# Two clears of 780 columns per group on GpSimd, between the row gathers of both edge stages

## What is computed

```python
# layer 0: attention over edges
h = (x @ W).reshape(N, H, C)
e = jax.nn.leaky_relu(a_src[src] + a_dst[dst], NEG_SLOPE)
e_exp = jnp.exp(e - e_max[dst])
out = jax.ops.segment_sum(h[src] * alpha[:, :, None], dst, num_segments=N)
# layer 1: messages from four products, weights from an MLP of the edge's 8 numbers
w = silu(edge_scalars @ fc_w1 * ...) @ fc_w2 * ...
xg0, xg1 = y0[edge_src], y1[edge_src]
agg = jax.ops.segment_sum(mids, edge_dst, num_segments=n)
```

## Time and profile before

| | us |
|---|---|
| median of 3 runs | 4372.39 |
| lowest, highest | 4357.10, 4376.29 |
| the profiled execution | 4357.34 |
| its span, first to last instruction | 4355.6 |
| mean granted TensorE clock | 0.833 |

### The profile page before, as it was taken

The page is one execution under the profiler, slowest core; times in us unless marked ns, Lnnn a source line. Parts: engine busy times, 40 slices in busy tenths (PEclk is TensorE's granted clock), DMA queues, the critical chain, the costliest instruction groups (busy, mean ns, idle before and its releaser), DMA issues. The chain is left out here.

```text
span 4355.6 us, 80354 instructions
## 1 busy us (share of the span) xinstructions
PE 3384.6 (78%) x22728; PEld 2463.9 (57%) x22728; DVE 2266.0 (52%) x6165; ACT 1433.0 (33%) x4367; POOL 1898.9 (44%) x2266
## 2 busy tenths in 40 slices
PE   6577777766777787999588888778887777878679
PEld 4466666655666665888344444444444444446568
DVE  5455555555555575766344444444444444456732
ACT  5122222222222173333133333333333333314612
POOL 3655656666556310111444444444444444451144
PEclk9678888888888898999678778887777877879889
DMA  6333333333333464322322222222222222223511
GB/s 196 109 88 84 86 85 91 87 85 87 84 87 93 105 191 127 92 85 75 91 66 67 64 65 67 68 67 64 65 65 66 66 64 66 67 80 97 172 42 48
DMA packets 239107, 375.93 MB, mean 86 GB/s; under 512 B 88190, under 2 KB 145606, under 8 KB 238762
## 3 DMA queue, kind: packets, MB, share of 16 engines
q0 software_dynamic: 89712, 230.26, 19.2%
q1 hardware_dynamic: 147482, 140.83, 11.6%
q10 hardware_dynamic: 1696, 2.62, 0.2%
HBM read 310.75 MB, written 62.84 MB: 86 GB/s over the span
## 5 line engine op out<-in xcount | busy, mean ns | idle before, releaser
L1980 POOL DMA_INDIRECT e_rows<-tab,e_ix x828 | 788.4, 952 | 1006.6 <-DVE e_msg L2154 679.5
L586 POOL DMA_INDIRECT e_rows<-tab,e_ix x830 | 794.0, 957 | 533.5 <-issue 254.2
L2222 PE MATMUL e_pU<-e_msg,e_oh 128*32 128x128 f32 (+1 forms) x6672 | 557.8, 337 | 312.2 <-issue 307.3
L2152 DVE TENSOR_TENSOR e_msg<-e_pW,e_rows 128x256 f32<-128x256 f32 x417 | 176.8, 424 | 925.3 <-remote 680.6
L2222 PEld LDWEIGHTS e_pU<-e_msg,e_oh 128*32 128x32 f32 x6672 | 297.7, 120 | 553.5 <-issue 495.0
L981 PE MATMUL e_pU<-e_ohp,e_rows 128*128 128x128 f32 x3340 | 531.8, 321 | 89.8 <-issue 85.9
L981 PEld LDWEIGHTS e_pU<-e_ohp,e_rows 128*128 128x128 f32 x3340 | 503.3, 235 | 103.6 <-issue 96.9
L2208 PE MATMUL e_pW<-e_w,e_hT 64*128 64x256 f32 x1668 | 396.8, 513 | 51.2 <-DVE e_msg L2154 22.4
L2154 DVE TENSOR_TENSOR e_msg<-e_pW,e_rows 128x384 f32<-128x384 f32 x834 | 422.2, 548 | 0.0
L695 ACT CAST e_ohT<-e_pT 64x640 bf16<-64x640 f32 x167 | 114.6, 686 | 900.0 <-remote 511.6
L2038 ACT COPY e_us<-e_pU 96x512 f32<-96x512 f32 x139 | 80.9, 582 | 752.4 <-PE e_pU L2222 653.3
(11 more groups left out here) (453 smaller groups left out, 5713.5 us busy)
## 6 DMA issues: line engine op xcount, KB each, us to landing
e_rows<-tab,e_ix POOLq DMA_INDIRECT x1658
xnT<-f_xnT SPq DMA_DIRECT2D x25, 250.0 KB, 3.2
e_xk<-xnT SPq DMA_DIRECT2D x25, 250.0 KB
xnT<-b_xT SPq DMA_DIRECT2D x25, 250.0 KB, 3.0
m_xnT<-xnT SPq DMA_DIRECT2D x25, 250.0 KB
xnT<-m_xT SPq DMA_DIRECT2D x25, 250.0 KB, 2.7
ffn_norm<-xnT SPq DMA_DIRECT2D x25, 250.0 KB
tab<-f_hrow SPq DMA_DIRECT2D x25, 227.5 KB
```

Source lines behind the costliest of these rows:

```text
L586: nc.gpsimd.indirect_dma_start(out=rows[:, s, j, :], out_offset=None, in_=env["tab0"], in_offset=bass.IndirectOffsetOnAxis(ap=at[:, j:j + ...
L1980: nc.gpsimd.indirect_dma_start(out=rows[:, r % PER, j, :], out_offset=None, in_=env["tab1"], in_offset=bass.IndirectOffsetOnAxis(ap=at[:, ...
L2222: last = nc.tensor.matmul(u8[:, 0:8:2, :] if c == 0 else u8[:, 1:2 + 2 * c:2 * c, :], oh[:, r % 2, ST * i + j, c, :], m[:, 0:4, :] if c == ...
```

## The change

In both edge stages GpSimd clears a tile of its own, `pace`, 128 partitions by 780 float32 columns, ahead of the first gather of each group (j = 0) and ahead of the fourth (j = 3). Nobody reads `pace`. Each clear increments a semaphore `s_pace`, and ahead of each clear but the first stands a hold until the clear before it is done. The clear for j = 0 stands behind the holds for the group's buffer, ahead of the hold for tile 0; the one for j = 3 stands ahead of the holds for tiles 3 and later, of the index copy and of the fourth gather. The two semaphores are reset with the others of their stage. Nothing is removed.

```diff
@@ edges0 @@
+        pace = sb("pace", [P, 780])
...
-        s_eq = sem("e0_equal")
+        s_eq, s_pace = sem("e0_equal"), sem("e0_pace")
...
                             hold(pool, s_acc, g - SLOTS + 1)
                         for j in range(GT):
+                            if j in (0, 3):
+                                if lo >= 1 or j == 3:
+                                    hold(pool, s_pace, 2 * g + j // 3)
+                                nc.gpsimd.memset(pace[:, :], 0.0).then_inc(s_pace, 1)
                             if lo >= 1:
                                 for i in ((j,) if j < 3 else range(3, GT) if j == 3 else ()):
                                     hold(pool, s_row[i], 16 * g)
@@ edges1 @@
+        pace = sb("pace", [P, 780])
...
+        s_pace = sem("e1_pace")
...
                             hold(pool, s_msg, PAIRS * (g - PER + 1))
                         for j in range(T1):
+                            if j in (0, 3):
+                                if lo >= 1 or j == 3:
+                                    hold(pool, s_pace, 2 * g + j // 3)
+                                nc.gpsimd.memset(pace[:, :], 0.0).then_inc(s_pace, 1)
                             if lo >= 1:
                                 for i in ((j,) if j < 3 else range(3, T1) if j == 3 else ()):
                                     hold(pool, s_row[i], 16 * g)
```

More of the change, by code:

```diff
@@ L1111, in edges0 @@
         window_loop(env, iota, one_pass, s_row, GROUPS,
-                    s_dw + [s_ix, s_oh, s_eq, s_T, s_ohT, s_E, s_lg, s_ed, s_p, s_ohp, s_acc, s_add,
+                    s_dw + [s_pace, s_ix, s_oh, s_eq, s_T, s_ohT, s_E, s_lg, s_ed, s_p, s_ohp, s_acc, s_add,
                             s_xk, s_kv, s_sq, s_ss, s_sd, s_kvn, s_ks, s_qw, s_wq, s_bp, s_kvb, s_pb,
@@ L2315, in edges1 @@
         window_loop(env, env["iotaW"][:, :], one_pass, s_row, GROUPS1,
-                    s_es + [s_ix, s_T, s_esT, s_F, s_h, s_W, s_msg, s_eq, s_oh, s_acc, s_us, s_flip, s_add,
+                    s_es + [s_pace, s_ix, s_T, s_esT, s_F, s_h, s_W, s_msg, s_eq, s_oh, s_acc, s_us, s_flip, s_add,
                             s_wk, s_xk, s_kv, s_read, s_ab, s_sd, s_ri, s_vs, s_gram, s_cp, s_wf, s_dT, s_M, s_m1, s_G, s_wl],
```

## The result

The changed kernel takes **4133.65 us** in the median of 4 runs (4120.31 to 4135.94); the kernel before took 4367.62 us beside it (4 runs). The ratio is 0.9459 with a 95% interval of 0.9428 to 0.949: 5.4% faster. The profiled execution took 4133.68 us with a span of 4131.9 us, 223.7 us less than before.

The account below looks back on a forecast made before the run. TensorE was taken as the busiest engine, held by "issue" stalls while row gathers are in flight. 4357.3 - 168 - 33 - 20 = 4136 us, plus 15 for the runs' median, said as 4150 us; range 3980 to 4390.

Parts of the forecast that it names:

- What GpSimd has to spare, and the clear's price: First stage, GpSimd: 1.8 of 8.2 us a group free; a clear costs 746 ns, making a group 7.75 us.
- The first stage, 33 us: First edge stage: relief of 0 to 66 us, where GpSimd stops it; half taken, 33 us.
- The waits, at nothing: GpSimd's waits on the pace semaphore are long met, and later gathers are wanted some four groups later: cost nil.
- The second stage's stall, 168 us: TensorE's "issue" idle in the second edge stage: relief of 0 to 337 us; half taken, 168 us.
- the clock, 20 us: TensorE's clock in the second stage rises as stalls get rarer: 0 to 142 us, 20 us taken.
- all of it: Upper bound of the second stage's relief: all 337 us of TensorE's idle time there.
- The `tensor_scalar`, at nothing: VectorE's L826 in the first stage could wait for clears: at most 125 us, 11 us on average, nothing taken.
- The cause: TensorE runs on a store of instructions that drains while row gathers are in flight; inferred from timing.
- Full relief: Rival: the break refills the store and almost no stall is left in either edge stage, 3920 us; chance 0.20.
- Only moved: Rival: each TensorE stall shifts 1.1 us and keeps its length, 4372 us; chance 0.17.
- GpSimd bound: Rival: GpSimd bounds the first stage, with no relief, at 8.93 us a group, +121 us, 4493 us; chance 0.11.

Follow-up runs that it names:

- first stage alone: Both clears in the first edge stage only, none in the second, against the kernel before: 4247.40 us, 0.9836.
- the first set: First of three sets of follow-up runs, each beside the kernel before, which took 4314.50 us in it.
- the third set: Last of three sets of follow-up runs, each beside the kernel before, which took 3344.69 us in it.
- the form with two inputs: VectorE's minimum as scalar_tensor_tensor, on the kernel with both clears in the first stage, the fourth gather's in the second (4110.78 us): 4106.39 us.
- the kernel with no-ops alone: The kernel before with 20 no-ops more on TensorE in each group of the second edge stage: 3341.09 us, 0.9989.
- The kernel with the double break: Against the kernel before: both clears in the first stage; in the second, two clears in a row ahead of the fourth gather only: 3965.44 us, 0.9084.
- the last kernel: Against the kernel before: both clears in the first stage; in the second, clears ahead of the third and fifth gathers: 3627.48 us, 1.0842.

## Why the prediction was right, and where it was not

The forecast was 4150 us and the runs gave 4134, inside the range. Direction and place of the gain were right, and so was the break inside the burst as what brings it. The terms of the second stage were each off and their errors cancelled, which is luck. By its steps:

- **What GpSimd has to spare, and the clear's price.** Right. A clear was priced at 746 ns and takes 758 to 763; the inner break is 1.05 us for 1.1. The group of 7.75 us on GpSimd showed as 7.72 us a group where the stage ran at its pace (first stage alone).
- **The first stage, 33 us.** It was 36, at 8.0 us a group with GpSimd 80% busy (forecast 8.0 and over 75%). "Issue" there fell by about 110 us (269 to 159), three times the gain; the rest went to TensorE's wait for one-hots, 124 to 185 us. The half that I took had no row behind it, and in the first set the same clears brought 64 us, nearly the whole 66 that I had as the bound, at GpSimd's pace; in the changed kernel GpSimd still had 52 us of idle time ahead of its clears. That 33 fits 36 is luck too.
- **The waits, at nothing.** No run changed them alone. Ahead of the clears GpSimd's idle time in the second stage is mostly for VectorE's messages (354 us), that is the buffer it waited for before (679.5 us). The later gathers are felt a little: VectorE's messages wait 60.2 us for gathered rows and not 25.3, but TensorE's wait for the messages did not grow (20.1 to 8.4 us).
- **The second stage's stall, 168 us, and the clock, 20 us.** Together 188, and the stage gave 187. Each was mis-sized. "Issue" fell by 213 us, not by 168. The idle time of TensorE fell by 47 us only, since ScalarE's late copy took 155 us. And the busy term was 139 us and not 20: it stood at the upper bound that I had worked out, 142 us, though for another reason in part. The rise of the clock from 0.79 to 0.82 gives, as an estimate, 1458 x (1 - 0.79/0.82) = 53 us; that the starved matmuls overlap again gives most of the rest, 99 us at the sums alone (the two shares cover each other in part). So the step that failed is the assumption that a stall is what "issue" shows and that its fall is gain. The bound of "all of it" failed with it: I had 337 us (the rows of the trace add up to 334), and without the stall the second stage is 701 us shorter, 1120.6 for 1821.6 us.
- **The `tensor_scalar`, at nothing.** Right, with the wait longer than I thought: a mean of 411 ns for 236, 29 us in all against my 11, and one of 1475 ns. Removing it changed nothing. In the third set it reached 138 us of VectorE's time, over the 125 us that I gave as its bound, and there too GpSimd set the stage's length. The Trainium skill (SBUF — State Buffer, section "Who interferes with whom") states a rule for it: a `tensor_scalar` in a 2-port mode and an instruction of GpSimd contend, and the one that comes second is blocked for the whole of the other. The runs agree: the form with two inputs takes 182 ns beside the same clears. The long ones exceed one clear; clear and index copy, which stand back to back, and its own 177 ns make 0.77 + 0.20 + 0.18 = 1.15 us, near the 1.18 us that is the median where the mean is 1091 ns.
- **The cause.** That TensorE runs on a store of instructions that drains was inferred, and no run shows it. What the runs show is wider. "Issue" on TensorE is one face of it, the "remote" waits of VectorE and ScalarE another. In the kernel with no-ops alone, in the third set, neither engine has such a row in the second stage: all of them vanish together. The same section of the Trainium skill says that "PE and ACT never wait on anyone". It speaks of the ports of SBUF; taken as my rival took it, that gathers cannot hold TensorE back, it fails in the first two sets and fits the third. Whether the engines waited at a port or for something else no run shows.
- **The rivals.** "Full relief" priced the stall at 337 us of idle plus 50 of clock, 3920 us. The kernel with the double break took 398 us off (4363.84 to 3965.44), and without the stall the kernel takes 3345 us, some 1000 less: there was far more to gain than my full relief held. "Only moved" is refuted by the kernel with the fourth gather's clear alone, in time and in "issue" (29.4 us at the sums), though a part of the stall did move, to ScalarE. "GpSimd bound" came true in the last kernel, with its mechanism and at +283 us, in the set without the stall. The changed kernel itself was not run there; the inner break alone (with the no-ops, which cost nothing by themselves) cost 3.5% there.

**What stays open.** Why gathers hold back the engines in some sets and not in another; whether descriptors, bytes or instruction traffic does it; whether two breaks are better than one long one where the stall is; and whether an idle pause of GpSimd would do as well as a clear, which was not tried. The first and the third set carry the same chip number, 15; whether it was the same chip is not known, so it isn't shown that the difference is one between chips.

## What to carry to other kernels

Where engines wait for "issue" or "remote" while indirect gathers are in flight, break the burst inside, not ahead of it, and try a longer break: 1.05 us inside took 5 to 6% off, 1.9 us in the second stage took 9%, and the clear ahead of the burst nothing by itself. Such a stall is larger than its idle rows: look at the busy time of the same matmuls and at the next engine's "remote" waits, and expect the wait to move there. Measure in more than one place and at more than one time before keeping such a pause. Where the stall is absent the clears cost their own time on a GpSimd that is then the bound: 3.5% with one a group, 8.4% with two.

## What the runs showed of the hardware

- The same program took 4368, 4315 and 4364 us in the median beside the changed kernel and in the first two sets, and 3345 us in the third, within 0.7% in each. Outside the two edge stages the executions agree: from the last gather of the one to the first of the other it is 626 us in the kernel before and 620 us in the one with no-ops alone. In the second edge stage the difference is 13.2 against 8.1 us a group, with TensorE at a clock of 0.79 against 0.95.
- While row gathers follow each other every 1.25 us, TensorE (9 matmuls in 5 us), ScalarE (2.2 us late at 2824.58) and VectorE (until 2819.03) can all stand still, and go on as the gathers end or pause; not in the third set.
- The granted clock follows the stall in the second stage: 0.79 with it, 0.82 with one break, 0.88 with the double one, 0.95 without it.
- A gather of 128 rows takes GpSimd 0.95 us, with rows of 1 KB or of a quarter of that; without a stall the first edge stage goes at its pace, 6.4 us a group of five. A GpSimd clear of 128 x 780 float32 takes 0.76 us, of 128 x 312 0.37 us and of 128 x 260 0.33 us.
